# Attention in phase B: score and side matmuls issued as four 32-column blocks, side steps in new places, gathers of six transfers

## The chip, the cores and the metric

One Trainium2 chip, one of its cores. The metric is the device time of one execution of the whole program in microseconds, the median of three runs. Lower is better.

## The reference, cut to what matters

The program is one layer of four parts, run one after the other: attention A, a feed-forward part, attention B, the feed-forward part again. The change touches attention B alone. Input there: x of 8 batches of 1024 tokens by 256 channels; 16 heads of 16 channels.

```python
inner = x @ (z / z_norm)
v = 2.0 * z_norm / c_sqrt * arcsinh(c_sqrt * lam * inner * cosh(two_cr) - (lam - 1.0) * sinh(two_cr))
w = sinh(c_sqrt * v) / c_sqrt
return w / (1.0 + sqrt(1.0 + c * sum(w * w, axis=-1, keepdims=True)))   # Q with z_q, K with z_k
...
V = x @ w_v.T + b_v
scores = einsum('bhqd,bhkd->bhqk', Qh, Kh) / sqrt(D_K)
probs = softmax(scores, axis=-1)
out = einsum('bhqk,bhkd->bhqd', probs, Vh)
```

x is the layer-normed input, and the result is added to the input before the norm.

## The kernel before

`phase_b` works batch by batch. Q and K (512 channels in all, four row tiles of 128 channels in `A` and `SQ`) are computed in float32 and split into three bf16 parts (`parts`), which go to a DRAM scratch (`store_parts`) and come back (`gather`) into `st`: for one group of four heads, 128 contraction rows are eight slices of 16 channels, so that one bf16 matmul with a contraction of 128 gives the float32-like product of Q and K of one head. `Q_PART` and `K_PART` say which part stands in which slice. `st` has two slots, for two of the four groups.

A batch is 32 blocks (`BLK`), 8 key tiles for each of 4 groups. A block has four units `j`, one for each head of the group:

- a unit's scores are two matmuls of 128 x 512 into `ps` (line 1956), which has room for two units, and then one exp of 128 x 1024 on ScalarE from `ps` to `pr` (line 1859). The scores of unit u wait for the exp of unit u - 2 (`probs_done`);
- after units 1 and 3 stands `weigh` of the block before (line 1938): for one half of the queries, four matmuls, one for each head, that each use 32 columns of the array and write 32 partitions of `acc`. It is float32, which the profile shows as two passes, so 8 records. It was in this four-block form already.

I call a half block what lies from one `weigh` to the next: two units and one `weigh`. A batch has 64 of them.

Between the units stands side work, which prepares the next batch: `STEPS` gives for each block the steps (kind, index, batch offset), and every engine walks through the same table and does its own part of a step. `inT` transposes the normed input (4 transposes per tile), `lamb` and `facb` broadcast a per-token factor with a matmul, `proj` is the projection, `v` the values, `sum` a sum over channels, `out` the transposes of a finished group; `square`, `root`, `ln`, `up`, `down` are ScalarE functions, and `stats`, `rstd`, `lam`, `y`, `sign`, `pair`, `fac`, `split`, `vaug` are done on VectorE and GpSimd. `UNIT_OF` spreads the tiles of a block over its units. Side tiles go to the two banks of `pm`, which VectorE empties (`misc_taken`). `PROLOGUE` is the same work for batch 0, ahead of the loop. Batches 1 to 5 are a hardware loop (`Fori`), 0, 6 and 7 are written out. SP issues all DMAs in order.

Of the kernel before, what the change touches and what calls it, by code (L numbers as in the profile page):

```python
# [21 lines left out]
P = 128  # L22
# [769 lines left out]
def phase_f(nc, tag, x_in, x_out, cn, gc, arange):  # L792
# [546 lines left out]
Q_PART = [0, 0, 0, 1, 1, 1, 2, 2]  # L1339
K_PART = [0, 1, 2, 0, 1, 2, 0, 1]  # L1340
# [25 lines left out]
    "pair1 sum1 fac0 facb0 facb1 split0 split2 split1 split3 vaug0 vaug1 vaug2 vaug3").split()] + \  # L1366
    [("stats", 0, 1), ("rstd", 0, 1), ("lam", 0, 1)]
UNIT_OF = {1: (2,), 2: (0, 2), 3: (0, 1, 3), 4: (0, 1, 2, 3)}
N_TILES = {"inT": 2, "lamb": 2, "proj": 1, "v": 1, "sum": 1, "facb": 2, "out": 2}


def steps_at(blk, first, left):

    return [(kind, i, off) for kind, i, off in STEPS.get(blk, [])
            if off <= left and not (first and (kind, i) in (("out", 3), ("vaug", 3)))]


def phase_b(nc, x_in, x_out, zq, bq, zk, bk, wvT, bv):
# [5 lines left out]
    scratch = nc.dram_tensor("b_scratch", [2, 3, D, T], BF16, kind="Internal").ap()  # L1384
# [5 lines left out]
    with Scope(nc, "b") as s:  # L1390
        passed = s.passed
        z_sb = s.sb("z", [P, 2, KD, D])
        wv_sb = s.sb("wv", [P, KD, D])
# [32 lines left out]
        names = ("w_loaded setup_p setup_v setup_a setup_m xl_loaded xr_loaded stored stats_done mv_done rstd_done "  # L1426
# [6 lines left out]
        N_W = 16 * 8  # L1433
        N_G = 16 * 16

        PRO = sum(N_TILES.get(kind, 0) for kind, _, _ in PROLOGUE)
        TILES = sum(N_TILES.get(kind, 0) for blk in range(BLK) for kind, _, _ in STEPS.get(blk, []))
        LATE = N_TILES["out"]

        LAST = sum(N_TILES.get(kind, 0) for blk in range(BLK) for kind, _, off in STEPS.get(blk, []) if off > 0)  # L1440

        def misc_base(b, first):

            return (PRO, PRO % 2) if first else (PRO - LATE + TILES * b, (PRO - LATE) % 2)
# [585 lines left out]
```

## Time and profile before

| | |
|---|---|
| median of 3 runs | 3173.93 us (3173.55 to 3176.45) |
| the profiled execution | 3171.44 us, of which the span from first to last instruction is 3169.6 us |
| mean granted TensorE clock | 0.962 |
| matmul busy (PE), ScalarE (ACT), VectorE (DVE), GpSimd (POOL) | 2838.4, 2026.5, 1846.0, 1273.0 us |
| attention B: from the first score matmul to the last | 1448.0 to 2772 us |
| DMAs | 200.30 MB, of them 512 of 128 KB in `gather` |

The profile has the four parts in a row: attention A, the feed-forward part to 1320 us, attention B to about 2775 us, the feed-forward part. PE counts matmuls (their ends are modelled, and they overlap), PEld weight loads. In a timeline, the first number is the start in us from the start of the span, the second the length of the merged piece, and x8 the number of instructions in it; in brackets stands the idle time of the engine before it and what ended it.

### The profile page before, as it was taken

What the parts mean: (1) busy time and instruction counts of PE and PEld (TensorE: products, weight loads), DVE (VectorE), ACT (ScalarE), POOL (GpSimd) and SP (SyncE); (2) the same over time, 40 slices, a digit from 0 to 9 for tenths busy, and PEclk for the clock granted to TensorE, in tenths of its full rate; (3) what the DMA queues carried; (4) which work ended last, traced back from release to release, by engine and by line L of the source; (5) the groups of instructions that cost most, each with busy time, mean ns of one, the idle gap of its engine ahead of it and who ended that gap; (6) DMA issues with size and microseconds to landing.
All of it is one profiled execution on the core that took longest, in us unless ns stands there. A gap on an engine that the chain in (4) does not pass through costs nothing. (4 is left out here: it accounts for less than half of the span.)

```text
span 3169.6 us, 38539 instructions
## 1 busy us (share of the span) xinstructions
PE 2838.4 (90%) x12161; PEld 1226.5 (39%) x12161; DVE 1846.0 (58%) x2420; ACT 2026.5 (64%) x2650; POOL 1273.0 (40%) x786
## 2 busy tenths in 40 slices
PE   3899999999979999657999999999999999969997
PEld 1455555555554444322323232323233332234443
DVE  8899999999973453454443444444444441144444
ACT  6454555455425555325889797978878889835554
POOL 4798899889861220141314131322313230021210
PEclk7899999999999999778999999999999999989999
DMA  2010001010012211206263635535553627231112
GB/s 80 1 37 27 30 26 36 23 33 26 24 56 75 80 53 53 67 11 132 29 146 42 134 54 94 93 73 92 92 94 58 116 46 128 27 114 48 60 53 67
DMA packets 163998, 200.30 MB, mean 63 GB/s; under 512 B 16504, under 2 KB 118272, under 8 KB 163840
## 3 DMA queue, kind: packets, MB, share of 16 engines
q1 hardware_dynamic: 163840, 198.25, 28.4%
q8 instruction: 92, 1.51, 0.2%
q14 instruction: 66, 0.54, 0.1%
HBM read 139.49 MB, written 58.72 MB: 63 GB/s over the span
## 5 line engine op out<-in xcount | busy, mean ns | idle before, releaser
L1859 ACT ACTIVATE b_pr<-b_ps 128x1024 f32<-128x1024 f32 x1024 | 1002.8, 1025 | 255.5 <-PE b_ps L1956 251.2
L1956 PE MATMUL b_ps<-b_st 128*128 128x512 bf16 x2048 | 591.2, 386 | 71.0 <-DMA b_st<-b_scratch 31.6
L1938 PE MATMUL b_acc<-b_pr,b_vaug 128*32 128x512 f32 x4096 | 549.0, 608 | 0.4 <-ACT b_pr L1859 0.4
L1956 PEld LDWEIGHTS b_ps<-b_st 128*128 128x128 bf16 x2048 | 150.3, 98 | 649.5 <-ACT b_pr L1859 381.9
L1257 PE MATMUL f_po<-f_s,f_w 128*128 128x512 f32 x768 | 355.0, 605 | 9.4 <-DVE f_xr L1042 5.9
L1030 DVE TENSOR_TENSOR f_turned<-f_cs,f_s 128x1024 f32<-128x1024 f32 x96 | 119.3, 1243 | 364.4 <-ACT f_cs L1159 359.4
L635 PE MATMUL a_pv<-a_xnT,a_wv 128*128 128x512 f32 x512 | 251.2, 614 | 52.8 <-DVE a_mem L403 38.7
L1123 ACT ACTIVATE f_h<-f_po,f_b 128x512 f32<-128x512 f32 x192 | 131.9, 687 | 218.1 <-PE f_po L1257 218.1
L627 PE MATMUL a_pu<-a_xnT,a_wk 128*128 128x512 f32 x512 | 238.3, 609 | 29.2 <-DVE a_frac L355 23.2
L1575 POOL TENSOR_TENSOR b_SQ<-b_A 128x1024 f32<-128x1024 f32 x32 | 64.7, 2021 | 467.1 <-DVE b_A L1672 467.1
L674 PE MATMUL a_py<-a_wo,a_out 128*128 128x256 f32 x960 | 229.1, 382 | 0.0
L1257 PEld LDWEIGHTS f_po<-f_s,f_w 128*128 128x128 f32 x768 | 141.4, 191 | 214.6 <-issue 160.8
L674 PEld LDWEIGHTS a_py<-a_wo,a_out 128*128 128x128 f32 x960 | 184.5, 192 | 25.8
L525 ACT ACTIVATE a_rnd<-a_frac 128x1024 f32<-128x1024 f32 x64 | 67.7, 1057 | 197.0 <-DVE a_frac L355 197.0
L1265 PE MATMUL f_po<-f_h,f_w 128*128 128x512 f32 x384 | 175.5, 600 | 2.6 <-PEq L1248 2.3
L523 ACT ACTIVATE a_rnd<-a_pu,a_cst 128x1024 f32<-128x1024 f32 x64 | 71.1, 1111 | 163.8 <-PE a_pu L627 163.8
L1748 DVE COPY b_osb<-b_acc 128x512 f32<-128x512 f32 x64 | 44.2, 691 | 218.0 <-PE b_acc L1938 210.6
L1938 PEld LDWEIGHTS b_acc<-b_pr,b_vaug 128*32 128x32 f32 x4096 | 81.0, 108 | 220.2 <-issue 207.9
L277 POOL TENSOR_TENSOR a_out<-a_mem,a_trig_k 128x1024 f32<-128x1024 f32 x64 | 139.6, 2182 | 54.8 <-DVE a_mem L415 54.8
L627 PEld LDWEIGHTS a_pu<-a_xnT,a_wk 128*128 128x128 f32 x512 | 99.9, 197 | 156.5 <-issue 130.5
L635 PEld LDWEIGHTS a_pv<-a_xnT,a_wv 128*128 128x128 f32 x512 | 95.9, 193 | 164.3 <-issue 83.3
L268 POOL TENSOR_TENSOR a_turn_c<-a_mem,a_trig_t 128x1024 f32<-128x1024 f32 x64 | 151.5, 2367 | 18.5 <-DVE a_mem L415 18.5
(259 smaller groups left out, 4694.4 us busy)
## 6 DMA issues: line engine op xcount, KB each, us to landing
b_st<-b_scratch SPq DMA_DIRECT2D x512, 128.0 KB, 7.0
b_scratch<-b_parts SPq DMA_DIRECT2D x32, 768.0 KB, 7.7
f_xl<-x SPq DMA_DIRECT2D x16, 1024.0 KB, 5.5
f_xr<-x SPq DMA_DIRECT2D x16, 1024.0 KB, 6.8
a_xl<-in_L_attn_a_x_dram SPq DMA_DIRECT2D x16, 512.0 KB, 4.2
x<-a_xr SPq DMA_DIRECT2D x32, 256.0 KB, 2.2
x<-f_xr SPq DMA_DIRECT2D x8, 1024.0 KB, 4.5
b_xl<-x SPq DMA_DIRECT2D x8, 1024.0 KB, 7.8
```

Of the source, the lines that this page charges most:

```text
L268: nc.gpsimd.tensor_tensor(halves(turn_c[:]), pair_of(s, 0), halves(cos_t[:, c, :]), ALU.mult).then_inc(turned, 1)
L277: nc.gpsimd.tensor_tensor(halves(o), pair_of(s, 2), of_tokens(cos_k[:, s, :]), ALU.mult).then_inc(turned, 1)
L627: i = nc.tensor.matmul(pu[:, h * 512:(h + 1) * 512], wk_sb[:, k, c * P:(c + 1) * P], xnT[:, k, h * 512:(h + 1) * 512], start=k == 0, stop= ...
L635: i = nc.tensor.matmul(pv[:, h * 512:(h + 1) * 512], wv_sb[:, k, c * P:(c + 1) * P], xnT[:, k, h * 512:(h + 1) * 512], start=k == 0, stop= ...
L674: i = nc.tensor.matmul(o, out[:, c, t * P:(t + 1) * P], wo_sb[:, c, :], start=False, stop=c == c0 + HC - 1)
L1030: nc.vector.tensor_tensor(turned[:, h], cs[:, x, c].unsqueeze(1).broadcast_to([P, KD, HT]), src[:, x, :, c], ALU.mult).then_inc(product_do ...
L1123: nc.scalar.activation(h1[:, x, m, h * HT:(h + 1) * HT], p, ACT.Gelu, bias=b1_sb[:, m:m + 1]).then_inc(act_done, 1)
L1257: q = nc.tensor.matmul(po[:, (at + t) % RING, :], w1_sb[:, f, m * P:(m + 1) * P], S[k][:, x, f, h * HT:(h + 1) * HT], start=f == 0, stop=f ...
L1265: q = nc.tensor.matmul(po[:, (at + h) % RING, :], w2_sb[:, f, :], h1[:, x, f, h * HT:(h + 1) * HT], start=f == 0, stop=f == KD - 1)
L1859: nc.scalar.activation(pr[:, 4 * (blk % 2) + j, :], ps[:, j % 2, :], ACT.Exp, scale=SC).then_inc(S["probs_done"], 1)
L1938: x = nc.tensor.matmul(acc[32 * j:32 * j + 32, h * 512:(h + 1) * 512], vaug[:, kt, c:c + 32], pr[:, 4 * (kt % 2) + j, h * 512:(h + 1) * 51 ...
L1956: x = nc.tensor.matmul(ps[:, j % 2, h * 512:(h + 1) * 512], st[:, g % 2, 1, j, kt * P:(kt + 1) * P], st[:, g % 2, 0, j, h * 512:(h + 1) * ...
```

## The change

It does these things:

- a helper `blocks` issues a matmul as four, each with 32 columns of the weights and 32 partitions of the result. Scores, `lamb`, `facb`, `proj`, `v` and `sum` go through it. The transposes (`inT`, `out`) stay 128 wide;
- `proj` becomes `proja` and `projb`, the two halves of the contraction, at units 0 and 2 of a block. Every step of `STEPS` now carries its unit, and a tile of `inT`, `lamb`, `facb`, `out` is a step of its own. The places change: `proj` stands in blocks 31 and 0 to 6, where it stood in 4 to 12; `inT`, `lamb` and the first `proj` are done a batch earlier (offset 2, blocks 25 to 31, and for batch 1 in the prologue); `out` of the last group moves from block 2 to 7; `v` to 8 to 15;
- the scratch has the head's 16 dimensions outside the four heads, `gather` issues six transfers of 48 or 32 partitions with rows of 8 KB instead of 16 of 16 partitions with rows of 2 KB, and to match, the columns of z are permuted once into `zp` on ScalarE at the start;
- `lamb` has a diagonal of its own (`dgl`), and SP issues the load of `xl` first in a batch.

```diff
-Q_PART = [0, 0, 0, 1, 1, 1, 2, 2]
-K_PART = [0, 1, 2, 0, 1, 2, 0, 1]
+Q_RUNS = [(0, 3, 0), (3, 3, 1), (6, 2, 2)]
+K_RUNS = [(0, 3, 0), (3, 3, 0), (6, 2, 0)]
...
 STEPS = {
-    3: [("lamb", 0, 1)], 4: [("proj", 0, 1), ("proj", 1, 1), ("vaug", 3, 0)], 5: [("proj", 2, 1)], 6: [("square", 0, 1), ("proj", 3, 1)],
+    3: [("root", 0, 1, 0), ("proja", 4, 1, 0), ("y", 0, 1, 0), ("projb", 4, 1, 2)],
+    4: [("square", 1, 1, 0), ("ln", 0, 1, 2), ("proja", 5, 1, 0), ("vaug", 3, 0, 0), ("projb", 5, 1, 2)],
...
-    scratch = nc.dram_tensor("b_scratch", [2, 3, D, T], BF16, kind="Internal").ap()
+    scratch = nc.dram_tensor("b_scratch", [2, 3, H // 4, DK, 4, T], BF16, kind="Internal").ap()
...
             slot = g % 2
-            for o, part in enumerate((Q_PART, K_PART)):
-                for i, w in enumerate(part):
-                    sp.dma_start(st[i * DK:(i + 1) * DK, slot, o],
-                                 scratch[o, w, 64 * g:64 * g + 64, :].rearrange("(h d) t -> d h t", d=DK))\
-                        .then_inc(st_loaded[slot], 16)
+            for i, n, w in Q_RUNS:
+                sp.dma_start(st[i * DK:(i + n) * DK, slot, 0].rearrange("p h t -> p (h t)"),
+                             scratch[0, w, g].rearrange("d h t -> d (h t)").unsqueeze(1).broadcast_to([DK, n, 4 * T]))\
+                    .then_inc(st_loaded[slot], 16)
+            for i, n, w in K_RUNS:
+                sp.dma_start(st[i * DK:(i + n) * DK, slot, 1].rearrange("p h t -> p (h t)"),
+                             scratch[1, w:w + n, g].rearrange("w d h t -> d w (h t)")).then_inc(st_loaded[slot], 16)
...
+                def blocks(o, w, v, start=True, stop=True):
+
+                    for r in range(0, P, 32):
+                        x = nc.tensor.matmul(o[r:r + 32], w[:, r:r + 32], v, start=start, stop=stop, skip_group_check=True)
+                    return x
...
-                    if kind == "proj":
+                    if kind in ("proja", "projb"):
+                        k = 0 if kind == "proja" else 1
...
                         q, c = i // 2, slice((i % 2) * 512, (i % 2 + 1) * 512)
-                        for k in range(KD):
-                            x = nc.tensor.matmul(bank, z_sb[:, q // 2, k, (q % 2) * P:(q % 2 + 1) * P], xnT[:, k, c],
-                                                 start=k == 0, stop=k == KD - 1)
+                        x = blocks(bank, zp[:, q // 2, k, (q % 2) * P:(q % 2 + 1) * P], xnT[:, k, c], k == 0, k == KD - 1)
...
                             for h in range(2):
-                                x = nc.tensor.matmul(ps[:, j % 2, h * 512:(h + 1) * 512],
-                                                     st[:, g % 2, 1, j, kt * P:(kt + 1) * P],
-                                                     st[:, g % 2, 0, j, h * 512:(h + 1) * 512], start=True, stop=True)
+                                x = blocks(ps[:, j % 2, h * 512:(h + 1) * 512], st[:, g % 2, 1, j, kt * P:(kt + 1) * P],
+                                           st[:, g % 2, 0, j, h * 512:(h + 1) * 512])
```

The program order of TensorE before, in the loop over batches, around a `proj` tile (`b_ps<-b_st` is a unit's scores, `b_pm<-b_xnT,b_z` the projection, `b_acc` the `weigh`):

```order
L1956 MATMUL b_ps<-b_st 128x512 [waits b_probs_done]
L1956 MATMUL b_ps<-b_st 128x512
L1873 REGISTER_ALU
L1900 MATMUL b_pm<-b_xnT,b_z 128x512 [waits b_misc_taken]
L1900 MATMUL b_pm<-b_xnT,b_z 128x512
L1954 REGISTER_ALU
L1956 MATMUL b_ps<-b_st 128x512 [waits b_probs_done]
L1956 MATMUL b_ps<-b_st 128x512
L1938 MATMUL b_acc<-b_pr,b_vaug 32x512 [waits b_probs_done]
L1938 MATMUL b_acc<-b_pr,b_vaug 32x512 x3
```

And of the change, at the end of a batch (`b_zp` is the permuted z):

```order
L1897 MATMUL b_ps<-b_st 32x512 [waits b_probs_done]
L1897 MATMUL b_ps<-b_st 32x512 x7
L1897 MATMUL b_pm<-b_xnT,b_zp 32x512 [waits b_misc_taken]
L1897 MATMUL b_pm<-b_xnT,b_zp 32x512 x3
L1897 MATMUL b_ps<-b_st 32x512 [waits b_probs_done]
L1897 MATMUL b_ps<-b_st 32x512 x7
L1963 MATMUL b_acc<-b_pr,b_vaug 32x512 [waits b_probs_done]
L1963 MATMUL b_acc<-b_pr,b_vaug 32x512 x3
L1897 MATMUL b_ps<-b_st 32x512 [waits b_probs_done]
L1897 MATMUL b_ps<-b_st 32x512 x7
L1897 MATMUL b_pm<-b_xnT,b_zp 32x512 x4
L1897 MATMUL b_ps<-b_st 32x512 [waits b_probs_done]
```

Every instruction between two `weigh` now has the shape of `weigh`, and one half of the projection stands in each half block where all of it stood in one.

SP's queue ahead of the first scores, before: a store of Q and K, the 16 transfers of group 0, the second store, the 16 of group 1:

```order
L1453 DMA b_scratch<-b_parts 128x3x1024
L1462 DMA b_st<-b_scratch 16x4x1024 [waits b_parts_stored0]
L1462 DMA b_st<-b_scratch 16x4x1024 x15
L1453 DMA b_scratch<-b_parts 128x3x1024 [waits b_parts_done]
L1453 DMA b_scratch<-b_parts 128x3x1024
L1462 DMA b_st<-b_scratch 16x4x1024 x16
```

The same place of the change:

```order
L1466 DMA b_scratch<-b_parts 128x3x1024
L1474 DMA b_st<-b_scratch 48x1x4096 [waits b_parts_stored0]
L1474 DMA b_st<-b_scratch 48x1x4096
L1474 DMA b_st<-b_scratch 32x1x4096
L1478 DMA b_st<-b_scratch 48x1x4096 x2
L1478 DMA b_st<-b_scratch 32x1x4096
L1466 DMA b_scratch<-b_parts 128x3x1024 [waits b_parts_done]
```

The same bytes are moved, in 6 instead of 16 instructions of the queue.

## Rows read from the trace of the kernel before

**Rows 1.** The page, 40 slices of 79 us: busy tenths.
```profile
PE   3899999999979999657999999999999999969997
...
ACT  6454555455425555325889797978878889835554
```

**Rows 2.** Windows, batches 0, 2, 6, 7: us, busy PE, PEld, DVE, ACT, POOL; clock, DMA.
```profile
1448.00:1612.60 164.60, 161.81 (x900) 51.08 (x900) 72.41 (x114) 143.38 (x148) 44.77 (x29) 0.99 0.43 80
...
1782.10:1954.30 172.20, 164.54 (x924) 52.88 (x925) 76.39 (x123) 143.19 (x148) 45.10 (x29) 0.99 0.48 86
...
2468.40:2633.90 165.50, 163.13 (x928) 52.26 (x925) 71.84 (x102) 143.75 (x149) 36.85 (x18) 1.00 0.46 78
2633.90:2772.20 138.30, 136.15 (x821) 29.80 (x817) 15.42 (x34) 124.43 (x129) 0.00 (x0) 1.00 0.43 70
```

**Rows 3.** Groups of batch 2: line, operation, count, busy us, mean ns.
```profile
L1859 ACT ACTIVATE b_pr<-b_ps 128x1024 f32<-128x1024 f32 x128 | 125.4, 1026 | 27.5 <-PE b_ps L1956 27.1
L1956 PE MATMUL b_ps<-b_st 128*128 128x512 bf16 x256 | 73.8, 385 | 6.2 <-issue 3.1 <-ACT b_pr L1859 1.3 <-PE b_pm L1883 0.3
L1938 PE MATMUL b_acc<-b_pr,b_vaug 128*32 128x512 f32 x512 | 69.1, 612 | 0.0
L1900 PE MATMUL b_pm<-b_xnT,b_z 128*128 128x512 f32 x32 | 15.0, 592 | 0.0
L1905 PE MATMUL b_pm<-b_wv,b_xnT 128*128 128x256 f32 x32 | 8.3, 382 | 0.0
L1892 PE MATMUL b_pm<-b_dg,b_ones 128*128 128x512 f32 x12 | 6.1, 592 | 0.0
L1923 PE MATMUL b_pm<-b_ident,b_osb 128*128 128x128 f32 x32 | 4.9, 276 | 0.0
...
L1911 PE MATMUL b_pm<-b_cst,b_A 128*128 128x1 f32 x32 | 3.7, 245 | 0.0
L1883 PE MATMUL b_pm<-b_ident,b_xl 128*128 128x128 f32 x16 | 2.5, 276 | 0.0
```

**Rows 4.** Timeline of batch 3: scores, a transposed tile, scores, weigh, scores.
```profile
1961.55 0.60 PE L1883 MATMUL b_pm<-b_ident,b_xl 128*128 128x128 f32 x4
1961.99 0.59 PE L1956 MATMUL b_ps<-b_st 128*128 128x512 bf16 x2
...
1962.51 0.16 PEld L1938 LDWEIGHTS b_acc<-b_pr,b_vaug 128*32 128x32 f32 x8 [0.42 <-issue]
1962.51 1.06 PE L1938 MATMUL b_acc<-b_pr,b_vaug 128*32 128x512 f32 x8
...
1963.51 0.61 PE L1956 MATMUL b_ps<-b_st 128*128 128x512 bf16 x2
...
1964.15 1.94 ACT L1859 ACTIVATE b_pr<-b_ps 128x1024 f32<-128x1024 f32 x2 [0.38 <-PE b_ps L1956]
```

**Rows 5.** Timeline of batch 3, PE alone: a half block with a proj tile.
```profile
1977.78 0.60 PE L1956 MATMUL b_ps<-b_st 128*128 128x512 bf16 x2
1978.22 1.88 PE L1900 MATMUL b_pm<-b_xnT,b_z 128*128 128x512 f32 x4
...
1981.46 0.60 PE L1956 MATMUL b_ps<-b_st 128*128 128x512 bf16 x2
```

**Rows 6.** Timeline of batch 7: weigh, two half blocks apart, without side work.
```profile
2720.17 1.06 PE L1938 MATMUL b_acc<-b_pr,b_vaug 128*32 128x512 f32 x8
...
2724.34 1.06 PE L1938 MATMUL b_acc<-b_pr,b_vaug 128*32 128x512 f32 x8
```

**Rows 7.** Timeline, first scores of batches 2 and 5, behind the loop's branch.
```profile
1782.10 1.05 PE L1956 MATMUL b_ps<-b_st 128*128 128x512 bf16 x4 [3.13 <-issue]
...
2300.08 1.89 PE L1956 MATMUL b_ps<-b_st 128*128 128x512 bf16 x4 [4.75 <-issue]
```

**Rows 8.** The page's DMA issues: count, KB each, us to landing.
```profile
b_st<-b_scratch SPq DMA_DIRECT2D x512, 128.0 KB, 7.0
```

**Rows 9.** Timeline ahead of batch 0: gather of group 0, last side work, first scores.
```profile
1431.31 7.37 SPq L1462 DMA_DIRECT2D b_st<-b_scratch  x16
...
1433.99 1.43 DVE L1702 COPY b_vaug<-b_vnew 128x512 f32<-128x512 f32 x4
...
1447.96 1.89 PE L1956 MATMUL b_ps<-b_st 128*128 128x512 bf16 x4 [31.60 <-DMA b_st<-b_scratch]
```

More of the change, by code:

```diff
@@ L1362 @@
-PROLOGUE = [(step[:-1], int(step[-1]), 0) for step in (
[3 rows of a table removed]
[L1366 to L1369, printed above, removed]
+    0: [("proja", 1, 1, 0), ("projb", 1, 1, 2)], 1: [("proja", 2, 1, 0), ("projb", 2, 1, 2)],
+    2: [("square", 0, 1, 0), ("proja", 3, 1, 0), ("projb", 3, 1, 2)],
@@ new lines @@
+    18: [("down", 3, 1, 0), ("out", 2, 0, 2)], 19: [("sign", 3, 1, 0), ("out", 3, 0, 2)],
+    20: [("pair", 1, 1, 0), ("sum", 1, 1, 2)], 21: [("fac", 0, 1, 0)],
+    22: [("facb", 0, 1, 0), ("facb", 1, 1, 2)], 23: [("facb", 2, 1, 0), ("split", 0, 1, 0)], 24: [("facb", 3, 1, 0)],
+    25: [("inT", 0, 2, 0), ("split", 2, 1, 0)], 26: [("inT", 1, 2, 0), ("out", 4, 0, 2)],
+    27: [("inT", 2, 2, 0), ("vaug", 0, 1, 0), ("out", 5, 0, 2)], 28: [("inT", 3, 2, 0), ("split", 1, 1, 0)],
+    29: [("lamb", 0, 2, 0), ("vaug", 1, 1, 0)], 30: [("lamb", 1, 2, 0), ("split", 3, 1, 0)],
@@ new lines @@
+    31: [("proja", 0, 2, 0), ("projb", 0, 2, 2), ("vaug", 2, 1, 0)]}
+PROLOGUE = [(step[:-1], int(step[-1]), 0) for step in (
[3 rows of a table added]
+    "up2 down2 ln3 sign2 v6 v7 up3 down3 sign3 pair0 sum0 pair1").split()] + [("stats", 0, 1)] + \
+    [(step[:-1], int(step[-1]), 0) for step in "sum1 fac0 facb0 facb1 facb2 facb3 split0 split2".split()] + \
+    [("rstd", 0, 1), ("lam", 0, 1)] + [(step[:-1], int(step[-1]), 0) for step in "split1 split3 vaug0 vaug1 vaug2 vaug3".split()] + \
+    [(step[:-1], int(step[-1]), 1) for step in "inT0 inT1 inT2 inT3 lamb0 lamb1 proja0 projb0".split()]
@@ L1372, in steps_at @@
+TILE_KINDS = ("inT", "lamb", "projb", "v", "sum", "facb", "out")
+PE_KINDS = TILE_KINDS + ("proja",)
+ACT_KINDS = ("square", "root", "ln", "up", "down")
 def steps_at(blk, first, left):
-    return [(kind, i, off) for kind, i, off in STEPS.get(blk, [])
-            if off <= left and not (first and (kind, i) in (("out", 3), ("vaug", 3)))]
+    return [(kind, i, off, at) for kind, i, off, at in STEPS.get(blk, [])
+            if off <= left and not (first and (kind, i) in (("out", 6), ("out", 7), ("vaug", 3)))]
@@ L1432, in phase_b, with misc_base @@
         st_loaded = [s.sem(f"st_loaded{i}") for i in range(2)]
[L1433 to L1444, printed above, removed]
+        N_W = 16 * 12
+        N_G = 16 * (len(Q_RUNS) + len(K_RUNS))
+        PRO = sum(kind in TILE_KINDS for kind, _, _ in PROLOGUE)
+        offs = [off for blk in range(BLK) for kind, _, off, _ in STEPS.get(blk, []) if kind in TILE_KINDS]
+        TILES, LATE = len(offs), offs.count(-1)
+        AHEAD, LAST = offs.count(2), offs.count(1) + offs.count(2)
+        assert TILES % 2 == 0
+        def misc_base(b, first=False, left=2):
+            skipped = 0 if first else LATE + (AHEAD if left == 0 else 0)
+            return (PRO - skipped + TILES * b, (PRO - skipped) % 2)
         def store_parts(sp, b, f):
@@ L1910, in step @@
                         for t in range(NT):
[L1911 to L1912 removed]
+                            x = blocks(bank[:, t:t + 1], A[:, 2 * i, t * P:(t + 1) * P], cst[:, 2:3])
                     x.then_inc(S["misc_ready"], 1)
[L1914 removed]
+                    if kind == "inT" and i == 3:
                         pe.wait_ge(S["misc_ready"], m + 1)
```

208 lines of the change are left out of this document (107 added, 101 removed), and 10 rows, old and new, of tables (PROLOGUE, STEPS).

## The prediction

> **What bounds the kernel now.** I read the page's slices first, then windows by batch, then the groups of one batch, then timelines. The slices say that from slice 18 on, attention B, TensorE is at nine tenths or more nearly everywhere and ScalarE at seven to nine [rows 1]. The windows make that sharp: in batch 2 PE is busy 164.5 of 172.2 us, ScalarE 143.2, VectorE 76.4, GpSimd 45.1 [rows 2]. So two engines are near the bound, and PE is the nearer one. But a busy PE row counts overlapping records, so I count what PE has to do from the spacing of its starts.
>
> A bf16 matmul of 512 columns takes 0.21 us: two of them last 0.59, of which the last alone is 0.385 [rows 3, 4]. A float32 pass of 512 columns takes 0.43: four last 1.88, the last alone 0.59 [rows 5]. A transpose takes 0.11: four last 0.60, the last 0.276 [rows 3, 4]. And `weigh`, two passes in four blocks, starts 0.52 after the scores ahead of it started, and the next scores start 1.00 after it [rows 4]. Two score matmuls are 0.43 and two passes 0.87, so 0.09 is lost going in and 0.13 coming out: 0.22 per `weigh`. That is not the change between bf16 and float32: from the transposes (float32, 128 wide) to the scores it is 0.44 for four of 0.11 [rows 4], so nothing is lost there. It comes with the change between 128 and 32 columns. Within `weigh`, all eight weight loads (0.108 each) are over in 0.16, and the second passes start 0.45 after the first one started, 0.43 but for the four blocks' own offsets (1.06 less the mean of 0.612) [rows 3, 4]. So four blocks together take as long as one wide pass (0.43), and their loads are hidden.
>
> PE's work in a batch [counts from rows 3], before: 256 scores at 0.215 are 55; 64 `weigh` at 0.87 + 0.22 are 70; `proj` 32 passes, `lamb` and `facb` 12, at 0.43, `v` 32 at 0.215, transposes 48 at 0.11, `sum` 3.7: 34.8. Sum 159.8, where a batch without the loop's branch takes 164.6 to 165.5 [rows 2]. PE is 97% taken. ScalarE: 128 exps that follow each other at 0.92 (two last 1.94, one 1.026 [rows 3, 4]) are 118, and the rest of its 143.2 busy us [rows 2, 3] is 18: 136. It is the second bound, 24 us away.
>
> **Part 1, the blocks.** Scores and side matmuls get `weigh`'s shape; transposes don't. The 64 changes in and out go: 64 x 0.22 = 14.1 us per batch. The 12 transposed tiles (`inT` 4, `out` 8) stood among 128-wide matmuls and now stand among narrow ones: 12 x 0.22 = 2.6 comes back. Net 11.5 of PE work per batch: 148.3.
>
> How much reaches the time depends on the half block. With side work, PE is the bound. A half block with a `proj` tile lasts 3.68 [rows 5] = 0.87 scores + 1.73 side + 0.87 + 0.22, and gives all 0.22. Without side work two half blocks last 4.17 [rows 6], and PE's own work is 2 x 1.95. There the chain goes through `weigh` once in two half blocks and the other time through the exps (scores of unit u wait for exp u - 2, and it starts 0.64 after its scores [rows 4]). So such a pair gains 0.22 once: 3.95, 0.11 for each half block.
>
> The new table has 16 half blocks with `proja` or `projb`, 8 `v`, 12 transposed, 6 `lamb` and `facb`, 2 `sum`: 44, and 20 plain. Gain: 44 x 0.22 + 20 x 0.11 - 2.6 = 9.3 us per batch.
>
> **Part 2, the places.** Before, eight half blocks of 3.68 were followed by plain ones, where PE could only follow ScalarE. Split in two, a pair is 2 x (1.73 + 0.87) = 5.20 instead of 3.68 + 1.97. That is 0.45 less, just two times 0.22, counted already. What the even spread gives beyond that is at most the idle rest: 165.5 - 159.8 = 5.7. ScalarE's steps now mostly stand in half blocks that have PE work too; there ScalarE takes 1.85 + 1.1 = 2.95 against PE's 2.60 for `proj` and 2.17 for `v`, so in some 18 half blocks it sets the pace and part of the gain isn't had, and the next half block gets some back. I take zero for the two together. Moving `inT`, `lamb` and the first `proj` a batch ahead costs nothing in batches 0 to 5, and takes 5.3 us of PE work out of batch 6 (4 x 0.44 + 2 x 0.87 + 1.73 = 5.2; before, batch 6 did it for 7).
>
> Sum over attention B: batches 0 to 5, 6 x 9.3 = 56; batch 6, 9.3 + 5.2 = 14; batch 7 (138.3 [rows 2], hardly any side work), 64 x 0.11 = 7. 77 us. The four waits at the loop's branch (two of them 3.1 and 4.8 us; behind the longer one PE runs at the lower clock, 1.2 GHz: four score matmuls last 1.89 [rows 7]) stay.
>
> **Part 3, the gathers.** They are hidden already, but for group 0 of batch 0: PE waits 31.6 us there; the 16 transfers take 7.37 us to issue and the scores start 16.6 after the first [rows 9]; 128 KB lands after 7.0 [rows 8]. With 6 issues of about 0.46 (7.37 / 16) and the same bytes it can land between 2.8 + 7 = 10 and 16.6 us later. But behind it stands new work: the eight tiles `inT0` to `projb0` of batch 1, which VectorE takes only after its splits and `vaug` (to 1435.4 [rows 9]). Seven copies of about 0.7 in turn with PE's passes at half clock, some 9 to 10 us, end near 1445. So the first scores come between 1445 and 1449, 1 us gained, the permutation of z and the longer list of loads (0.5 us issue each, 4 more) taking up to 2 back: I take -1 to +2 and 0 as value. In the loop a faster gather only lands earlier. SP's queue: store and load of `xr` now wait for block 7 instead of 2, ahead of group 2's gather, which has 7 blocks (35 us) of room.
>
> **Against my price.** The one price that no row shows is four blocks of bf16. The nearest row is `weigh`: its passes are 0.43, like a wide one's. From the same bytes per us I take 0.215. The other end is that a narrow pass costs 0.43 whatever the type: 2048 x 0.215 = +440 us. Between them, each 0.01 us costs 20 us, so the gain is gone at 0.215 + 77 / 2048 = 0.253.
>
> The Trainium skill (TensorE: Matmul & The Clock Gate, Part 3, measured speedup) gives three column tiles of 512 columns a speedup of 2.38, not 3. By that a group takes 1.26 times a pass, 0.27 for the scores, and the sum would be 77 - 2048 x 0.056 = 38 us slower; the trace has 1.00 for float32, and its number decides. The skill also says (TensorEngine Tiling (Array Packing), Gotcha 2) that column tiling excludes the fast weight load.
>
> **Rivals.**
> 1. *The shared pass is longer* (slower). If a bf16 block group takes 0.27 (a factor of 1.26 on 0.215), attention B is 2048 x 0.056 - 77 = 38 us longer: 3212. It decides from 0.253. The rule of the paragraph above would be this. Against it stands `weigh`'s factor of 1.00.
> 2. *PE is fed too slowly.* A batch has 924 matmuls with their loads now [rows 2], and 1024 + 512 + 4 x 108 + 48 = 2016 in the change. At 82 ns per pair the gain is gone (165.5 / 2016); at 90, +16 us per batch: 3290. Against it: eight loads and eight matmuls of `weigh` are accepted inside 0.16 us [rows 4].
> 3. *A side step is late in its new place.* Candidates: `facb` in block 22, only 1.5 blocks after `sum1`, with a pow and two diagonals of GpSimd between; `sum1` half a block after `pair1`; ScalarE waiting for GpSimd at `square`. Each would stop PE or the exps once per batch for 1 to 4 us, seven times: 10 to 30 less gained, 3115. For it: the chains are tight on paper. Against: VectorE and GpSimd are under half busy.
> 4. *More than PE's work.* If the idle 5.7 us goes too, 35 more: 3060. Against: ScalarE's 136 and the chain through the exps.
>
> **Numbers.** Sum: 77 for the blocks and places, 0 ahead. The profiled execution, 3171.4, gives 3094; the median of the runs is 2.5 above it, so 3173.9 - 77 = 3097. Chances: forecast (3080 to 3110) 0.6; late steps (to 3135) 0.17; more gained (to 3055) 0.12; longer pass or feed 0.1; nothing 0.01. Range: the bounds of part 3 and rivals 3 and 4 make 3060 to 3135. What a measurement of this kernel can tell is about 0.2%, 6 us. Faster 0.9, same 0.02, slower 0.08.
>
> **What would show it.** In the profile after: 128*32 score records; `weigh` to next scores 0.87 instead of 1.00; two plain half blocks in 3.95; `proj` half blocks 2.60; batches of 155 to 157 us and the last of 131; around a transposed tile 0.65 for 0.44 of work. Wrong: spacing of the scores' block groups above 0.22; PE idle "issue" inside half blocks; ScalarE or PE idle on `b_dg`, `b_SQ` or `b_A` in batches.

## The result, and the profile after

The changed kernel takes 3091.13 us (median of four runs, 3084.2 to 3096.91), the kernel before 3175.19 beside it. The ratio is 0.9732, 95% interval 0.9708 to 0.9756. 3097 was forecast. The sum was near the truth; four of its parts were not, and the sections below take it apart.

The page of the profiled execution (3095.4 us, span 3093.6) has the instruction queue, the groups that answer to [rows 3], now over all eight batches, and the gathers that answer to [rows 8]:

```profile
q8 instruction: 158, 2.59, 0.4%
...
L1878 ACT ACTIVATE b_pr<-b_ps 128x1024 f32<-128x1024 f32 x1024 | 1000.9, 1035 | 180.3 <-PE b_ps L1897 174.7
L1897 PE MATMUL b_ps<-b_st 128*32 128x512 bf16 x8192 | 617.1, 383 | 53.1 <-ACT b_pr L1878 26.4
L1963 PE MATMUL b_acc<-b_pr,b_vaug 128*32 128x512 f32 x4096 | 534.5, 596 | 3.7 <-DVE b_osb L1763 3.3
...
b_st<-b_scratch SPq DMA_DIRECT2D x128, 384.0 KB, 8.1
```

The windows of batches 0, 2, 3, 6 and 7 answer to [rows 2]: us, busy PE, PEld, DVE, ACT, POOL with counts, clock, DMA share, GB/s.

```profile
1452.20:1604.60 152.40, 147.08 (x1996) 52.16 (x1992) 76.23 (x115) 142.11 (x148) 46.20 (x29) 1.00 0.36 82
1764.60:1929.60 165.00, 152.09 (x2020) 53.80 (x2022) 78.17 (x123) 143.25 (x148) 46.02 (x29) 0.99 0.37 92
1929.60:2097.10 167.50, 154.89 (x2020) 54.74 (x2024) 78.10 (x123) 143.21 (x148) 45.09 (x29) 0.97 0.37 90
2417.90:2568.30 150.40, 144.98 (x1976) 50.96 (x1972) 70.05 (x96) 141.81 (x149) 36.81 (x17) 1.00 0.39 97
2568.30:2697.10 128.80, 123.20 (x1572) 39.09 (x1564) 14.73 (x33) 121.68 (x129) 0.00 (x0) 1.00 0.30 67
```

Read the columns in turn. PE's matmul records per batch went from 924 to 2020. ScalarE's busy time is what it was. And two batches with nearly the same work take 152.4 and 167.5 us: batch 0 is written out, batch 3 is in the loop. Two more `out` tiles in batch 3 are 1.4 us of that (e3 below); the other 14 us of the loop aren't work.

Inside a batch the spacing is as priced. The last batch, PE, answers to [rows 6]; start and length in us:

```profile
2652.25 1.03 PE L1963 MATMUL b_acc<-b_pr,b_vaug 128*32 128x512 f32 x8
2653.11 1.15 PE L1897 MATMUL b_ps<-b_st 128*32 128x512 bf16 x16
2654.08 1.03 PE L1963 MATMUL b_acc<-b_pr,b_vaug 128*32 128x512 f32 x8
2654.94 0.60 PE L1897 MATMUL b_ps<-b_st 128*32 128x512 bf16 x8
...
2656.20 1.03 PE L1963 MATMUL b_acc<-b_pr,b_vaug 128*32 128x512 f32 x8
```

From `weigh` to the next scores 0.86 (1.00 in [rows 4]), and two plain half blocks 3.95 (4.17 in [rows 6]). Half blocks with a projection pass, start of batch 1, answer to [rows 5]:

```profile
1606.36 1.03 PE L1963 MATMUL b_acc<-b_pr,b_vaug 128*32 128x512 f32 x8
1607.22 0.60 PE L1897 MATMUL b_ps<-b_st 128*32 128x512 bf16 x8
1607.65 1.03 PE L1897 MATMUL b_pm<-b_xnT,b_zp 128*32 128x512 f32 x8
1608.51 0.60 PE L1897 MATMUL b_ps<-b_st 128*32 128x512 bf16 x8
1608.94 1.03 PE L1963 MATMUL b_acc<-b_pr,b_vaug 128*32 128x512 f32 x8
```

A half block is 2.58: 0.86 for `weigh`, 0.43, 0.86 for a projection pass, 0.43, and nothing lost between them.

What isn't work shows in two places. Batch 2 ends at the loop's branch (compare [rows 7]):

```profile
1922.74 0.60 PE L1897 MATMUL b_ps<-b_st 128*32 128x512 bf16 x8
1923.17 1.03 PE L1963 MATMUL b_acc<-b_pr,b_vaug 128*32 128x512 f32 x8
1929.58 1.04 PE L1897 MATMUL b_ps<-b_st 128*32 128x512 bf16 x8 [5.38 <-issue]
1930.41 1.07 PE L1897 MATMUL b_pm<-b_xnT,b_zp 128*32 128x512 f32 x4
```

PE stands still for 5.38 us and goes on at its lower clock (the eight score matmuls, from 1929.58 to 1930.41, take 0.83 where they take 0.43 otherwise). And in the midst of batch 2, in the midst of one `v` tile, after 5 of its 16 matmuls:

```profile
1822.90 0.60 PE L1897 MATMUL b_ps<-b_st 128*32 128x512 bf16 x8
1823.33 0.60 PE L1897 MATMUL b_pm<-b_wv,b_xnT 128*32 128x256 f32 x5
1827.39 0.84 PE L1897 MATMUL b_pm<-b_wv,b_xnT 128*32 128x256 f32 x10 [3.46 <-issue]
```

No semaphore stands between two matmuls of one tile, so the likely lack is instructions. Two views of the transfers fit that, of 1808 to 1824.4 and of 1824.4 to 1828 (queue: packets, MB, share of the 16 engines):

```profile
DMA  0000399999990000475899999989999699997999
...
q1 hardware_dynamic: 2293, 3.45, 80.2%
```

```profile
q1 hardware_dynamic: 120, 0.72, 97.5%
q8 instruction: 1, 0.02, 2.7%
```

For 16.4 us there is no packet of the instruction queue q8 at all, while the store and load of `xr` and the gather of group 2 run. The DMA engines are idle to 1809.6 and from 1812.9 to 1814.5, and no packet starts there either; if one was held back, it was from then on. PE goes on 3 us after the packet. But long spacing alone makes no stop: in the same trace no packet starts between 1732.7 and 1749.9, and PE runs on.

Such a packet has 16 KB (158 are 2.59 MB). The Trainium skill (Trainium Architecture — The Big Picture, The software stack) says that an instruction has 64 bytes, so a packet would be 256 of them. The trace agrees: the whole program has 17,472 more matmul and load records than before (20,897 of each for 12,161), and 66 packets more (158 for 92) are 256 x 66 = 16,900 instructions. A batch of attention B has 4042 such records where it had 1849 [rows 2]. A batch of 160 us now wants a packet every 9 to 10 us.

### The profile page after: what moved, and what is told of

Read it like the earlier page. It is cut to its first block and busy times, and to the rows that moved or that the text cites. A ratio compares the mean times of both kernels' runs of the same rounds, so it can differ in the third digit from the quotient of the medians.

```text
span 3093.6 us, 55718 instructions
## 1 busy us (share of the span) xinstructions
PE 2736.1 (88%) x20897; PEld 1234.7 (40%) x20897; DVE 1872.1 (61%) x2420; ACT 2023.4 (65%) x2651; POOL 1279.7 (41%) x786
## 3 DMA queue, kind: packets, MB, share of 16 engines
q8 instruction: 158, 2.59, 0.4%
## 5 line engine op out<-in xcount | busy, mean ns | idle before, releaser
L1897 PE MATMUL b_ps<-b_st 128*32 128x512 bf16 x8192 | 617.1, 383 | 53.1 <-ACT b_pr L1878 26.4
L1963 PE MATMUL b_acc<-b_pr,b_vaug 128*32 128x512 f32 x4096 | 534.5, 596 | 3.7 <-DVE b_osb L1763 3.3
L1897 PEld LDWEIGHTS b_ps<-b_st 128*32 128x32 bf16 x8192 | 180.2, 96 | 614.6 <-ACT b_pr L1878 362.6
L1963 PEld LDWEIGHTS b_acc<-b_pr,b_vaug 128*32 128x32 f32 x4096 | 125.4, 111 | 112.5 <-DVE b_osb L1763 6.8
L414 DVE TENSOR_TENSOR_SCAN a_po<-a_mem,a_po 128x512 f32<-128x512 f32 x128 | 156.6, 1223 | 2.2
```

The source lines that it names most:

```text
L414: nc.vector.tensor_tensor_scan(po[:, 1, :], mem[:, s, i, 1, :], po[:, 1, :], 0.0, ALU.add, ALU.add).then_inc(sin_scanned, 1)
L1897: x = nc.tensor.matmul(o[r:r + 32], w[:, r:r + 32], v, start=start, stop=stop, skip_group_check=True)
L1963: x = nc.tensor.matmul(acc[32 * j:32 * j + 32, h * 512:(h + 1) * 512], vaug[:, kt, c:c + 32], pr[:, 4 * (kt % 2) + j, h * 512:(h + 1) * 51 ...
```

## The experiments

In all of them a batch is counted from its first exp to the first exp of the next, in the profiled execution; attention B runs to 0.6 us behind the start of its last exp. Each ratio is to the kernel before as run beside that kernel (medians 3169.2 to 3175.2). Batch 0, written out and free of stops in most kernels (not in e2, e6 and e11), is the clean sample.

| kernel | median us | ratio to before (95%) | batch 0 | batches 1 to 5 | batch 6 | batch 7 | all |
|---|---|---|---|---|---|---|---|
| before | 3175.2 | 1 | 164.3 | 855.7 | 165.5 | 135.3 | 1320.8 |
| changed | 3091.1 | 0.9732 (0.9708 to 0.9756) | 152.6 | 813.1 | 150.4 | 128.3 | 1244.3 |
| e1 new table, wide | 3151.6 | 0.9926 (0.9909 to 0.9942) | 161.4 | 844.4 | 159.2 | 134.6 | 1299.6 |
| e2 old table, blocks | 3163.5 | 0.9969 (0.9957 to 0.9981) | 161.8 | 861.7 | 166.5 | 129.9 | 1319.8 |
| e9 side tiles wide | 3167.6 | 0.9981 (0.9971 to 0.9991) | 161.3 | 867.3 | 158.3 | 128.3 | 1315.1 |
| e10 proj whole | 3109.7 | 0.9799 (0.9782 to 0.9815) | 156.0 | 831.9 | 152.3 | 128.3 | 1268.5 |
| e12 sum wide | 3099.3 | 0.9758 (0.9738 to 0.9778) | 155.0 | 807.9 | 152.8 | 128.3 | 1244.0 |
| e3 changed, written out | 3047.8 | 0.9603 (0.9587 to 0.9619) | 152.5 | 769.5 | 150.4 | 128.3 | 1200.6 |
| e4 late gather | 3082.2 | 0.9708 (0.9691 to 0.9724) | 152.5 | 800.4 | 150.3 | 128.3 | 1231.5 |
| e5 old gathers | 3088.6 | 0.9746 (0.9722 to 0.9769) | 152.5 | 806.9 | 152.0 | 128.3 | 1239.7 |
| e6 sixteen transfers | 3091.3 | 0.9743 (0.9727 to 0.9759) | 155.7 | 797.7 | 150.6 | 128.5 | 1232.6 |
| e7 before, written out | 3148.7 | 0.9925 (0.9908 to 0.9941) | 164.2 | 828.5 | 165.5 | 135.3 | 1293.5 |
| e11 e2 written out | 3123.5 | 0.9848 (0.9831 to 0.9866) | 162.8 | 814.9 | 162.7 | 129.4 | 1269.7 |
| e13 e3 with old gathers | 3055.2 | 0.9637 (0.9616 to 0.9659) | 152.4 | 769.5 | 151.8 | 128.6 | 1202.2 |

The code ahead of attention B, which no kernel here changes, ends between 1314 and 1320 us in these traces. From there to the first exp it is 131 to 138 us, and behind the last exp 396 to 400. These spreads are in the whole times and not in the columns of batches.

**e1, the new table alone.** `blocks` issues one wide matmul:

```
-                    for r in range(0, P, 32):
-                        x = nc.tensor.matmul(o[r:r + 32], w[:, r:r + 32], v, ...)
-                    return x
+                    return nc.tensor.matmul(o, w, v, ...)
```

> The changed kernel with its whole new table of steps, its gathers and its prologue, but `blocks` issues one matmul of 128 columns instead of four of 32. My theory (the gain is the changes between 128 and 32 columns, the places are worth zero): 77 us slower than the changed kernel, near 3168, no different from the kernel before (3175) by more than 10 us; weigh to next scores 1.00 again, plain pair 4.17. Rival (the even spread of the side steps and the faster gathers bring a good part): 3130 or less. Third possibility (the new places alone cost something that the blocks hide): above 3185.

Measured 3151.6. Between the theories: the table (with its gathers) isn't worth zero, it brings 21 us of attention B, of which 5 were forecast (the work taken out of batch 6), but far from half of 77.

**e2, the blocks alone.** The kernel before, with scores, `lamb`, `facb`, `proj`, `v` and `sum` through `blocks`.

> The kernel before with nothing changed but the shape: scores, lamb, facb, proj, v and sum as four blocks of 32 columns; old table, old gathers, old prologue. My theory: the change of shape alone brings the work of 11.5 us of PE per batch, of which about 9 reach the time in batches 0 to 6 and 7 in the last; without the 5 us that the new table takes out of batch 6: 3175 - 70 = 3105, range 3095 to 3115. Half blocks with a whole proj tile 3.46 instead of 3.68. Rival (the blocks alone only expose ScalarE, and the new table is needed to use them): 3130 to 3150.

Measured 3163.5: 12 us, not 70. My theory fell here. Batch 0 has 161.8, of which 2.95 is one stop of PE at its end, so 158.9: without that stop the blocks bring 5.4 in the old table, and they bring 8.8 in the new one (161.4 to 152.6). The stop is a wait for data: the last of the 16 transfers of the next batch's group 0 lands at 1613.0, and PE goes on at 1613.15. The table brings 2.9 with wide matmuls and 6.3 with blocks, and takes that wait away besides. So the two parts depend on each other, and in the loop the blocks even cost 6 us.

**e9, scores in blocks, side tiles wide.**

```
-                        x = blocks(bank, zp[...], xnT[:, k, c], k == 0, k == KD - 1)
+                        x = side(bank, zp[...], xnT[:, k, c], k == 0, k == KD - 1)
```

and so for `lamb`, `facb`, `v` and `sum`, with `side` one matmul of 128 columns.

> The changed kernel with the scores in four blocks, and lamb, facb, proj, v and sum 128 columns wide again: 32 wide tiles per batch in half blocks that are narrow otherwise. My theory (0.09 in and 0.13 out, 0.22 us per wide tile): half blocks with proj and no ScalarE step 2.80 instead of 2.58; of the 32 tiles some 14 stand beside a step of ScalarE that hides it, so 18 x 0.22 = 4 us per batch, 28 in all, 3119; with all 32 of them 3140. Rival (what counts is only scores beside weigh, a wide side tile costs nothing more): 3091, or a few us less, for 648 PE instructions fewer per batch.

Measured 3167.6, nearly the whole gain gone, where 3119 was expected. PE in this kernel, a projection pass between narrow ones:

```profile
1952.40 0.61 PE L1897 MATMUL b_ps<-b_st 128*32 128x512 bf16 x8
1952.93 1.13 PE L1902 MATMUL b_pm<-b_xnT,b_zp 128*128 128x512 f32 x2
1953.99 0.61 PE L1897 MATMUL b_ps<-b_st 128*32 128x512 bf16 x8
```

0.53 from scores to tile (0.43 is work) and 1.06 from tile to scores (0.86 is work): 0.10 in and 0.20 out, 0.30 instead of my 0.22. The half blocks with a projection pass are 2.89 instead of 2.58. 161.3 in batch 0, against 161.4 with everything wide: blocks for the scores alone bring nothing, since each wide side tile pays the two changes again. In the loop this kernel is 23 us longer than e1 (867.3 for 844.4): PE stops for 6.2 to 7.4 us at the branch, and its granted clock is at 1.2 GHz for 10 to 14 us behind that. Of the 8.7 us that blocks for the side tiles bring, 2.4 are two half blocks with `sum`.

**e12, only `sum` wide.**

> The changed kernel with the two sum tiles of a batch (eight matmuls of one streamed column, 128 columns wide) wide again and all else narrow. My prediction priced a wide tile among narrow ones at 0.22 us, whatever is in it: 0.44 per batch, 3095. Theory L (a matmul of one streamed column takes as long as its weight load, and the load of 128 columns is dearer than four of 32): the two half blocks are 0.97 and 1.44 us longer, as in the run with all side tiles wide, 2.4 per batch, 3091 + 19 = 3110.

Batch 0 is 2.4 longer (152.6 to 155.0), as theory L had it; the price of 0.44 falls. PE around `sum` 1, first in the changed kernel, then here:

```profile
1552.43 0.69 PE L1897 MATMUL b_pm<-b_cst,b_A 128*32 128x1 f32 x62
...
1553.39 1.07 PE L1963 MATMUL b_acc<-b_pr,b_vaug 128*32 128x512 f32 x8
```

```profile
1556.04 1.95 PE L1937 MATMUL b_pm<-b_cst,b_A 128*128 128x1 f32 x16
1557.91 0.62 PE L1897 MATMUL b_ps<-b_st 128*32 128x512 bf16 x8
```

Sixteen wide matmuls of one column take 1.87 us to the next scores, 0.12 each; 64 narrow ones start within 0.55 us (two of them fall behind the row shown), 0.035 for a group of four. The whole kernel is only 8 us longer, not 19, and the intervals of the two ratios overlap. In the profiled executions attention B isn't longer at all (1244.0 for 1244.3): batches 0 and 6 are 2.4 longer each and the looped batches 5 shorter. No stop in mid-batch is left in this trace, and the program is 190 PE records per batch shorter. So the price of `sum` rests on the batches without a loop; the looped ones are disturbed by what e3 and e4 show.

**e10, a projection's two passes together,** `proja` at unit 2 with `projb`:

```
-    0: [("proja", 1, 1, 0), ("projb", 1, 1, 2)], 1: [("proja", 2, 1, 0), ("projb", 2, 1, 2)],
+    0: [("proja", 1, 1, 2), ("projb", 1, 1, 2)], 1: [("proja", 2, 1, 2), ("projb", 2, 1, 2)],
```

and so for the others.

> The changed kernel with the two passes of each projection tile together again: proja moves from unit 0 of its block to unit 2, beside projb; all else as in the changed kernel. My prediction's price (the split is worth 0.45 us per pair of half blocks when wide and next to nothing when narrow: 3.44 + 1.83 = 5.27 instead of 2 x 2.58 = 5.16): 8 x 0.1 us per batch, 3091 + 6 = 3097. Theory P (the place is worth more where a step of ScalarE stands in the same block: there the pair becomes 2.85 + 3.44 = 6.3 instead of 5.16, in five of the eight blocks): 5.5 us per batch, 3091 + 40 = 3131, range 3120 to 3140.

Measured 3109.7; batch 0 is 3.4 longer, batches 1 to 5 3.8 each. Neither price was right, but the place is worth 3.4 us and not 0.8. ScalarE and PE in block 1 of batch 0 show how, first here, then in the changed kernel (same exps, same ScalarE step `square`):

```profile
1454.25 1.89 PE L1897 MATMUL b_pm<-b_xnT,b_zp 128*32 128x512 f32 x16
...
1454.48 1.02 ACT L1878 ACTIVATE b_pr<-b_ps 128x1024 f32<-128x1024 f32 x1 [0.18 <-PE b_ps L1897]
...
1456.62 1.03 ACT L1878 ACTIVATE b_pr<-b_ps 128x1024 f32<-128x1024 f32 x1 [1.12 <-PE b_ps L1897]
...
1457.55 1.14 ACT L1850 ACTIVATE b_SQ<-b_SQ,b_cst 128x1024 f32<-128x1024 f32 x1
...
1458.59 2.84 ACT L1878 ACTIVATE b_pr<-b_ps 128x1024 f32<-128x1024 f32 x3
...
1459.65 0.62 PE L1897 MATMUL b_ps<-b_st 128*32 128x512 bf16 x8 [0.47 <-ACT b_pr L1878]
```

```profile
1459.35 1.03 ACT L1878 ACTIVATE b_pr<-b_ps 128x1024 f32<-128x1024 f32 x1 [0.26 <-PE b_ps L1897]
...
1460.64 1.03 ACT L1878 ACTIVATE b_pr<-b_ps 128x1024 f32<-128x1024 f32 x1 [0.26 <-PE b_ps L1897]
...
1461.56 1.14 ACT L1850 ACTIVATE b_SQ<-b_SQ,b_cst 128x1024 f32<-128x1024 f32 x1
...
1462.60 2.94 ACT L1878 ACTIVATE b_pr<-b_ps 128x1024 f32<-128x1024 f32 x3
```

With the whole tile in one half block ScalarE idles 1.12 us behind it. Then its own step comes, and PE idles for ScalarE. The two delays don't overlap: with two banks of scores neither engine can work ahead by more than two units. Split, the idle piece is 0.26 and PE's side work runs while ScalarE does its step. From exp to exp the half block is 4.11 here and 3.25 in the changed kernel.

**e3, the loop written out.** On every engine:

```
-                with pe.Fori(1, B - 2) as b:
+                for b in range(1, B - 2):
                     batch(b)
```

> The changed kernel with the loop over batches 1 to 5 of attention B written out on every engine, so that no branch is left there. Two kinds of PE waits stand in the changed kernel: four of 5.0 to 5.6 us at the loop's branch, and one of up to 3.5 us in the middle of each looped batch, in the midst of a v tile, with no semaphore behind it, ended 0.5 to 3 us after a 16 KB packet of the instruction queue. Theory F (both come from fetching instructions after a branch): batches 1 to 5 get as short as batch 0, 152.5 us, where they are 160.0, 165.0, 167.5, 163.1, 157.7 now: 51 us less, 3040. Theory D (only the waits at the branch are its doing; the one in mid-batch is an instruction packet that waits behind a burst of data transfers): the four waits and the slow clock behind them go, 4 x 6 to 8, about 28 less, 3063, and the waits in mid-batch stay. If neither: 3091.

Measured 3047.8, 43 less than the changed kernel: the best version of this study, better than both. The window of its batch 1 (columns as above, the clock the third from the end):

```profile
1599.10:1753.00 153.90, 149.78 (x2023) 53.72 (x2019) 80.16 (x124) 142.99 (x149) 46.24 (x29) 1.00 0.39 97
```

Each of batches 1 to 5 is 153.9 now, and batch 6 is 150.4 as before. Both kinds of stops are gone, as theory F said; of the 8 us that are missing to its 3040, 7 are because a batch of the middle has 1.4 us more than batch 0 (two more tiles).

**e4, the gather of group 2 four blocks later,** the loop as it was:

```
-                        sp.wait_ge(S["scores_ready"], 4 * BLK * b + 32 * (g - 1))
+                        sp.wait_ge(S["scores_ready"], 4 * BLK * b + (48 if g == 2 else 64))
```

> The changed kernel with the gather of group 2 issued when the scores of block 12 begin instead of block 8, so that its 2 MB don't follow in one burst on the store and load of x (2 MB) of block 8; the loop stays. Theory D (in mid-batch the instruction packet waits behind this burst): the half blocks of 3.13, 6.25, 6.52, 3.40 and 3.13 us at block 9 or 10 of batches 1 to 5 become 2.2 to 2.6 again, 9 to 12 us less, 3081. Theory F (instruction fetch is late there because of the loop, whatever the data): they stay, 3091. Either way the waits at the branch stay at 5.0 to 5.6.

Measured 3082.2. From exp to exp the longest half block in mid-batch was 6.65 us; none is over 3.25 now. Batches 1 to 5 lose 12.7 us, and the waits at the branch stay (5.0 to 5.7 us; 5.0 to 5.6 in the changed kernel). Its q8 has a packet at that place again, at 1818.1 where the changed kernel's came at 1824.5. The transfers from 1808 to 1822:

```profile
q1 hardware_dynamic: 2080, 2.10, 45.6%
q8 instruction: 1, 0.02, 0.5%
```

So the stop in mid-batch of this kernel needs both: the loop (e3) and the burst of 4 MB (e4). F foresaw e3 and failed here, D foresaw this run and failed in e3; neither alone is the whole.

**e7 and e11, the loop of the old table written out,** without and with blocks.

> The kernel before with the loop over batches 1 to 5 of attention B written out on every engine. If the waits at the branch there (3.1 to 4.8 us, and the slow clock behind them) are all that the loop costs: batches 1 to 5 as batch 6, 165.4 each, where they are 855 together: 28 less, 3147. If the loop's cost has nothing to do with the doubled number of PE instructions it is as large as in the changed kernel, where writing out brought 43 us: 3132. If the records at the branch mislead: 3175.

> The kernel before with blocks of 32 columns for scores and side work (as in the run of that alone), and its loop over batches 1 to 5 written out. Against the kernel before with the loop written out, 3149. Undisturbed half blocks gained 5.4 us per batch there in batch 0. If all the rest of what the blocks should have brought was lost at the loop's branches: 3149 - 45 = 3104. If PE still stands still in mid-batch for 3 to 5 us with no semaphore behind it, as in the written-out batches 0 and 6: 3130, range 3120 to 3140. If my step was right (9.3 per batch): 3085.

Measured 3148.7 and 3123.5. The loop cost the kernel before 27.2 us in batches 1 to 5 (855.7 to 828.5) and costs the changed one 43.6 (813.1 to 769.5), 16.4 more. Of the 43.6, e4 took back 12.7 by moving a gather, so the stops in mid-batch are most of the difference, and the longer stops at the branch the other 3.7.

e11 still has seven stops of 1.3 to 4.8 us with no branch in its program, and they are of two kinds. Three (3.13, 2.49 and 1.88) stand ahead of a batch's first scores and end within 0.1 us of the landing of group 0's last transfer. The first, which lands at 1612.1:

```profile
1612.17 1.05 PE L1878 MATMUL b_ps<-b_st 128*32 128x512 bf16 x16 [3.13 <-DMA b_st<-b_scratch]
```

All such waits together are 9.5 us in attention B. With blocks PE comes to the end of a batch sooner, and in the old table the old gather is then the last to be ready; the changed kernel has no such wait. That the new transfers and places took it away is read from these traces; no run has the old table with blocks and the new gathers. The other four stops are in mid-batch, with no semaphore behind them. The longest, PE:

```profile
2195.62 1.02 PE L1944 MATMUL b_acc<-b_pr,b_vaug 128*32 128x512 f32 x4
...
2201.46 1.07 PE L1944 MATMUL b_acc<-b_pr,b_vaug 128*32 128x512 f32 x2 [4.82 <-issue]
```

and the transfers from 2179 to 2198.2, then from 2198.2 to 2203.1:

```profile
DMA  0000000003899999999999999999999999989999
...
q1 hardware_dynamic: 1206, 1.99, 82.6%
```

```profile
q1 hardware_dynamic: 74, 0.10, 18.3%
q8 instruction: 2, 0.03, 3.4%
```

One gather of sixteen transfers fills the engines for 15 us; no instruction packet of q8 starts in 19 us, and PE stops in the middle of a `weigh`. The next packet starts as the gather ends. That the gather holds it back is read from these times; no run moved this gather. Batch 1 of e11 has no such stop and takes 160.2 where e7 has 166.4.

**e5, e6 and e13, the transfers.** e5 puts back the old scratch order, loads and gathers; e6 keeps the new order but issues sixteen transfers; e13 is e5 with the loop written out.

```
-            for i, n, w in K_RUNS:
-                sp.dma_start(st[i * DK:(i + n) * DK, slot, 1].rearrange("p h t -> p (h t)"), ...
+            for o, part in enumerate(([0, 0, 0, 1, 1, 1, 2, 2], [0, 1, 2, 0, 1, 2, 0, 1])):
+                for i, w in enumerate(part):
+                    sp.dma_start(st[i * DK:(i + 1) * DK, slot, o], ...
```

> The changed kernel with the old transfers alone: scratch in its old order, z copied without the permutation, a gather of sixteen transfers of 16 partitions with rows of 2 KB, the old loads of the biases. In the kernel before with blocks alone, PE stood still once or twice per batch for 2.5 to 4 us with no semaphore behind it, in written-out batches too. Theory D (a packet of PE instructions, wanted every 9 us now, waits behind the long gathers of 2 KB rows): such waits appear in batches 0 and 6 too and grow in the loop, 3 to 5 us per batch, 3091 + 25 = 3116, range 3105 to 3130. My prediction's price (a gather in the loop only lands earlier, zero): 3091.

> The changed kernel with its new scratch order and rows of 8 KB, but each gather as sixteen transfers of 16 partitions instead of six of 48 and 32. If what counts for the time is the size of the rows (few long packets instead of many short ones): 3091, within 6. If it is the number of transfers and how few partitions each has: as with the old gathers, 3105 or more; the first gather then also lands 5 us later.

> The changed kernel with its loop written out (3047.8 alone) and with the old transfers too: scratch in its old order, gathers of sixteen transfers of 16 partitions with rows of 2 KB. In the kernel before with blocks and a written-out loop, PE stopped in four or five of the eight batches for 1.3 to 4.8 us while a packet of instructions came late, 15 to 19 us after the one ahead of it, behind such a gather. Theory D (long gathers make instructions late, and the short ones of the changed kernel hide that): such stops come in the new table too, 1 to 3 us per batch, 3048 + 16 = 3064, range 3054 to 3074. My prediction's price (zero): 3048, with no stop.

e5 and e6 measure 3088.6 and 3091.3: no difference, theory D's 3116 fell. e13 measures 3055.2 against 3047.8, with intervals of the ratio that overlap. Its trace has 1.6 us more in attention B, and theory D's late instructions aren't in it: its two stops, 2.7 us ahead of the very first scores and 1.2 ahead of batch 7's, both wait for group 0's gather. The second:

```profile
2522.54 1.05 PE L1892 MATMUL b_ps<-b_st 128*32 128x512 bf16 x16 [1.21 <-DMA b_st<-b_scratch]
```

In the loop it is less clean. Which kernel's packets meet a gather is a matter of how its addresses and times fall, and I can't price it ahead: e6 has a stop of 1.4 in batch 0 (a half block of 4.44 from exp to exp) and shorter looped batches than e5.

## Why the prediction was right, and where its steps were not

- **Price of the blocks, 0.215 us for four of bf16: right.** Rival 1 is out. The trace doesn't bear out the rule of the Trainium skill (TensorE: Matmul & The Clock Gate, Part 3, measured speedup) of 2.38 for three column tiles: in this stream four take one wide pass, 0.43 in float32 and for two bf16 groups, a factor of 1.00.
- **Changes of shape, 0.22 per `weigh`: right there, too small elsewhere.** 0.86 and 3.95 were forecast as 0.87 and 3.95, 2.58 as 2.60. Around a wide float32 tile it is 0.30 (e9), around a transposed tile 0.69 for 0.44 of work where 0.65 was forecast (half block 2.42 less 1.73).
- **"`sum` 3.7": the term was mis-sized.** I carried it over unchanged. Narrow it is 2.4 us per batch less (e12).
- **"I take zero for the two together" (part 2): wrong.** The split of proj alone is 3.4 us per batch (e10), since ScalarE's steps and PE's tile made each other wait in turn. I had counted such half blocks by the slower engine's work; it is the two delays, one after the other, that cost. The blocks are worth only 5.4 in the old table, where 29 of the 64 half blocks of batch 0, from exp to exp, change by less than 0.03 us when made narrow (e2 against before). That this has the same reason is argued, not tested.
- **"The four waits at the loop's branch stay": wrong.** They grew from 3.1 to 4.8 us to 5.0 to 5.6, and stops in mid-batch came; together 16.4 us over batches 1 to 5, 3.3 per batch (e3 against e7), 12.7 of them the stops in mid-batch (e4). That is rival 2 in another form. Its price was 90 ns for each pair, everywhere; what the traces show is a few stops while a packet of instructions is awaited.
- **Part 3, -1 to +2: within the range, by other terms than mine.** From the last matmul of the code ahead to the first scores it is 133.7 before and 132.8 after, a gain of 0.9. By time from the start the first scores are 4 us later only because the unchanged code ahead ended 5.1 us later. Before, the scores wait for the gather, which lands at 133.7; after, it lands at 131.0 and PE's side work comes last, as I had it. With the old transfers (e5) the scores wait again, to 132.6. The new set's first gather is issued 2.7 us later than that one's (118.3 for 115.6, behind the permutation and the longer list of loads), and lands 12.7 after its first issue instead of 16.9, so the set as a whole brings nothing. Sixteen transfers in the new order (e6) land at 137.0: six instead of sixteen are worth 4.2 us at this one place.
- **"They are hidden already" (the gathers after the first): right in the new table, by e5 and e6,** but for 1.5 us that e5 waits ahead of batch 7. With blocks in the old table it isn't so: e11 waits 9.5 us for them in attention B.
- **The sum.** Batch 0 gained 11.7: 3.4 for the split and 2.4 for `sum` leave 5.9 for the changes of shape and the rest, where I had 9.3 for all. Looped batches gained 42.6 / 5 = 8.5: 11.8 of work, less 3.3 for feeding. Batch 6 gained 15.1 (14 forecast), batch 7 7.0 (7). So batches without stops are 152 to 154 us, where 155 to 157 were forecast. 11.7 + 42.6 + 15.1 + 7.0 = 76.4, against 77. The total agrees because two things not seen brought about 6 per batch (part of which I had given to the changes of shape) and a third took 3.3. That these errors cancel to within 1 us is luck, and the total is no proof of the working. The shares also assume that the prices of e10 and e12 add.

What stays open: how the fetch of instructions decides when to ask for a packet. In the looped kernel the same place of the program stops in batch after batch, and the written-out one never stops there with the same transfers beside it; I have no run that shows the step between. Nor does the size of the loop's body alone set the stop at the branch: e2, with about as many instructions as the changed kernel, has 5.7 to 6.5 us, e9 with fewer 6.2 to 7.4, and e12 2.8 to 5.2.

## What to carry to other kernels

When two engines hand work to each other through two buffers, count a step's place and not only its length: a long side step of one engine and one of the other in the same short stretch can cost both delays, and here splitting PE's brought 3.4 us per batch where I had counted nothing. A change of form pays when all neighbours take it: blocks for all brought 60 us (e1 to the changed kernel), for the scores alone nothing (e1 to e9, 16 us longer). And a faster engine meets transfers that were early enough before: look for waits that end as a transfer lands.

If an edit doubles an engine's instructions, look at the instruction queue in the profile and at the loop's branch before anything else: writing the loop out brought 43 us here, where it was worth 27 before, and it is the version to keep.

## What the runs showed of the hardware

- A float32 matmul of 128 columns of weights and one streamed column costs 0.12 us; four of 32 columns together 0.035 (e12 and the changed kernel). In e12 the sixteen weight loads start as far apart as the matmuls and fill the 1.86 us, so the load seems to set it.
- PE's instructions come in packets of 16 KB over the DMA engines that move data. Beside 4 MB of transfers none started for 16.4 us, beside one gather of small rows for 19 us, and PE stood still for 3.5 and 4.8 us, between two matmuls of one tile. Moving the one gather took the first of these stops away (e4); the second is not tested. A spacing of 17 us also passed without a stop.
- At the loop's branch PE stopped for 5.0 to 5.6 us with 4221 PE instructions in the loop's body (register ones included), 3.1 to 4.8 with 2036, but not in step with the size in other kernels. PE's granted clock stood at 1.2 GHz for the next 3 to 7 us. It also did behind the stop of 2.9 us in the middle of batch 3, and did not behind the one of 3.5 in batch 2. Written out (e3), the clock's column is 1.00 in every batch.
